# Filling TensorE's pauses at the start, and one low half moved from DVE to POOL at the end, in a recommendation tower

## The reference

```python
x0 = xk = e                                       # [b, 39, 16]
for idx, (W, b) in enumerate(params):             # W: (39, 39 or 64, 128)
    z = relu(einsum('bhd,bkd,hks->bsd', x0, xk, W) + b)
    # layers 0 and 1: xk = first 64 rows, the last 64 go to the output; layer 2: all 128
logit = sum(concatenate(direct, axis=1), axis=-1)  # [b, 256]
h = relu(concatenate([logit, dense_ctx]) @ W_top1 + b_top1)   # 272 -> 512
h = relu(h @ W_top2 + b_top2)                      # 512 -> 256
y = h @ W_top3
```

## Time and profile before

| | |
|---|---|
| median of 3 runs | 2482.67 us (2478.63, 2482.67, 2483.8) |
| the profiled execution | 2464.91 us, its span 2463.1 us |
| PE busy | 2416.9 us, 98% of the span, 8890 records |
| DVE busy | 2226.4 us, 90% |
| POOL busy | 1947.7 us, 79% |
| ACT busy | 1731.9 us, 70% |
| mean granted TensorE clock | 0.994 of full speed |

### The profile page before, as it was taken

One profiled execution on the slowest core, in us unless ns is written; L12 is line 12 of the kernel. 1 busy time (PEld: TensorE's weight loads), 2 busy tenths in 40 slices (PEclk: granted clock), 3 DMA queues, 4 the chain that ended last, 5 costly groups with the idle time before them and its releaser, 6 DMA issues.

```text
span 2463.1 us, 33434 instructions
## 1 busy us (share of the span) xinstructions
PE 2416.9 (98%) x8890; PEld 1646.8 (67%) x8890; DVE 2226.4 (90%) x1898; ACT 1731.9 (70%) x2202; POOL 1947.7 (79%) x1331
## 2 busy tenths in 40 slices
PE   6999999999999999999999999999999999999989
PEld 2566666666666666666666666666666666666656
DVE  1799999999989999999999999899999999999993
ACT  1677777777767777767777776676777777677655
POOL 6888888888878888888888888788887888866550
PEclk9899999999999999999999999999999999999999
DMA  3867766866766866776686677577678667767730
GB/s 76 182 140 157 165 136 140 175 140 136 163 139 128 172 146 137 155 162 139 138 175 139 138 161 158 118 163 154 137 148 174 134 139 168 148 138 150 164 93 1
DMA packets 214716, 352.60 MB, mean 143 GB/s; under 512 B 34382, under 2 KB 47566, under 8 KB 214588
## 3 DMA queue, kind: packets, MB, share of 16 engines
q1 hardware_dynamic: 194717, 347.07, 65.6%
q0 software_dynamic: 19968, 5.15, 2.2%
HBM read 346.97 MB, written 5.12 MB: 143 GB/s over the span
## 4 chain that ended last, share of the span: by engine, by line
PE 58%; POOL 24%; issue 13%; DVE 3%; ACT 1%; DMA 0%; POOLq 0%; SPq 0%; ACTq 0%; DVEq 0%
PE ps L929 22%; PE ps L939 11%; POOL Pl L422 11%; PE ps L919 10%; POOL emb L416 10%; PE ps L907 8%; PE ps L902 3%; POOL dir L451 2%; DVE P L764 1%; POOL sqx L428 1%; DVE ps L764 1%; PE ps L1056 1%; DVE Pl L769 1%; PE ps L895 1%; PE ps L1066 1%
## 5 line engine op out<-in xcount | busy, mean ns | idle before, releaser
L422 POOL TENSOR_TENSOR Pl<-P,Ph 128x1024 fp32r<-128x1024 f32 x448 | 1074.5, 2398 | 277.3 <-ACT Ph L566 268.8
L929 PE MATMUL ps<-Ph,wh 128*128 128x512 f32 x2048 | 965.0, 471 | 9.5 <-ACT Ph L566 9.5
L566 ACT ACTIVATE Ph<-ps 128x1024 fp32r<-128x1024 f32 x576 | 590.3, 1025 | 406.8 <-DVE ps L764 399.2
L764 DVE TENSOR_TENSOR P<-xb,ps 128x1024 f32<-128x1024 f32 x704 | 854.6, 1214 | 5.1 <-DMA xb<-x_dram 5.1
L769 DVE TENSOR_TENSOR Pl<-ps,Ph 128x1024 fp32r<-128x1024 f32 x576 | 705.4, 1225 | 112.8 <-ACT Ph L566 95.3
L929 PE MATMUL ps<-Ph,wl 128*128 128x512 f32 x1920 | 755.5, 394 | 0.0
L939 PE MATMUL ps<-Pl,wh 128*128 128x512 f32 x2048 | 742.4, 444 | 8.4 <-POOL Pl L422 8.4
L416 POOL DMA_INDIRECT emb<-tbl_in,idx x624 | 596.3, 956 | 171.5 <-issue 146.6
L764 DVE TENSOR_TENSOR ps<-xb,ps 128x1024 f32<-128x1024 f32 x576 | 707.0, 1227 | 19.6 <-DMA xb<-x_dram 1.3
L566 ACT ACTIVATE Ph<-P 128x1024 fp32r<-128x1024 f32 x448 | 473.9, 1058 | 186.0 <-DVE P L764 167.6
L939 PEld LDWEIGHTS ps<-Pl,wh 128*128 128x128 f32 x2048 | 384.5, 189 | 200.9 <-issue 117.9
(11 more groups left out here) (94 smaller groups left out, 899.3 us busy)
## 6 DMA issues: line engine op xcount, KB each, us to landing
xb<-x_dram SPq DMA_DIRECT2D x1280, 256.0 KB, 6.8
emb<-tbl_in,idx POOLq DMA_INDIRECT x624
x_dram<-rows SPq DMA_DIRECT2D x64, 78.0 KB
xb<-w_in SPq DMA_DIRECT2D x16, 128.0 KB
xb<-wt_in SPq DMA_DIRECT2D x2, 512.0 KB, 4.7
xb<-dense_in SPq DMA_DIRECT2D x1, 768.0 KB, 5.2
wp<-w_in SPq DMA_DIRECT2D x4, 128.0 KB
xb<-w0a_in SPq DMA_DIRECT2D x1, 448.0 KB
```

Source lines behind the costliest of these rows:

```text
L422: pool.tensor_tensor(Pl[:, h_slot(ref, c, k)], P[:, p_slot(ref, c, k)], Ph[:, h_slot(ref, c, k)], ALU.subtract).then_inc(low_pool, 1)
L566: act.activation(Ph[:, h_slot(ref, c, k)], p, ACT.Copy).then_inc(rounded, 1)
L764: dve.tensor_tensor(p, xb[:, x], xk.unsqueeze(1).broadcast_to([128, 2, N]), ALU.mult)\
L929: pe.matmul(z_of(c, k), w[:, q, j, :], Ph[:, h_slot(ref, c, k), j, :], start=k in (L1B, L2) and i + j == 0, stop=False)
```

## The change

Three edits.

1. The loop at the start becomes 80 products of 128x128 instead of 38 of 128x512, and the same short products are also issued in the loop over g: `WARM_T[g]` = 1 and 4 behind the transposes, `WARM_S[g]` = 1 and 2 behind the first three sums.
2. For chunk 1, ACT copies `x2` before `rows_sb` as it does for chunk 0; TensorE waits for `first_x` before the first two sums and for `aux_read` only before the third, which overwrites `aux_ps`.
3. The last chunk gets its own letters: step 10 goes from V to G, step 11 from G to V, step 12 from V to G. So of its steps 10 to 19, DVE makes 4 low halves instead of 5 and POOL 5 instead of 4.

```diff
-WARM = 38
+WARM, WARM_T, WARM_S = 80, (1, 4), (1, 2)
 KIND = "GVPVGPVGVPVGVGVGVGVP"
+LAST_KIND = "GVPVGPVGVPGVGGVGVGVP"
...
+def kind(i, k):
+    return (LAST_KIND if i == CHUNKS - 1 else KIND)[k]
...
             act.wait_ge(rows_written, 16)
-            copy_x(0, AUX)
+            act.wait_ge(aux_ready, AUX + 1)
+            act.activation(x2[:, :], aux_ps[0:R2], ACT.Copy).then_inc(first_x, 1)
+            act.activation(rows_sb, aux_ps[0:NF], ACT.Copy).then_inc(rows_ready, 1)
+            act.wait_ge(rows_ready, 2)
+            act.sem_inc(aux_read, 1)
...
-            with pe.Fori(0, WARM // 2):
-                for i in range(2):
-                    pe.matmul(z1_ps[:, 0], wp[:, 0, 0, :], wp[:, 0:2].rearrange("p q j m -> p (q j m)"), start=True, stop=True)
-
+            def repeat(n):
+                for i in range(n % 2):
+                    pe.matmul(z1_ps[:, 0, 0:S], wp[:, 0, 0, :], wp[:, 0, 1, :], start=True, stop=True)
+                if n < 2:
+                    return
+                with pe.Fori(0, n // 2):
+                    for i in range(2):
+                        pe.matmul(z1_ps[:, 0, 0:S], wp[:, 0, 0, :], wp[:, 0, 1, :], start=True, stop=True)
+
+            repeat(WARM)
...
                 transposes(g)
-                if g:
-                    pe.wait_ge(aux_read, READS + 1)
-                else:
-                    pe.wait_ge(first_x, 1)
+                repeat(WARM_T[g])
+                pe.wait_ge(first_x, g + 1)
                 for i, t in enumerate((FULL0, 0, 1)):
-                    if i == 2 and not g:
-                        pe.wait_ge(aux_read, 1)
+                    if i == 2:
+                        pe.wait_ge(aux_read, READS * g + 1)
                     sums(t, early_ps[g][i])
+                repeat(WARM_S[g])
```

More of the change, by code:

```diff
@@ L69 @@
                                              if not (i == CHUNKS - 1 and L1B <= k < L2)]
+def kind(i, k):
+    return (LAST_KIND if i == CHUNKS - 1 else KIND)[k]
+assert all((a == "P") == (b == "P") for a, b in zip(KIND, LAST_KIND))
 def counts(kinds):
@@ L76, in counts @@
         for k in range(STEPS):
-            n += KIND[k] in kinds and (i, k) in STEPSET
+            n += kind(i, k) in kinds and (i, k) in STEPSET
             table[i, k] = n
@@ L83 @@
 STEP, SPLITS, ONPOOL, ONDVE, PLAINS, STORED = (counts(kinds) for kinds in ("GVP", "GV", "G", "V", "P", "GP"))
-STORED_STEPS = [o for o in ORDER if KIND[o[1]] != "V"]
+STORED_STEPS = [o for o in ORDER if kind(*o) != "V"]
 SPLIT_STEPS = [o for o in ORDER if KIND[o[1]] != "P"]
@@ L483, in tile @@
                     for k in range(STEPS):
-                        if KIND[k] == "G" and (CPT * ref + c, k) in STEPSET:
+                        if kind(CPT * ref + c, k) == "G" and (CPT * ref + c, k) in STEPSET:
                             low(T, ref, c, k)
@@ L564, in round_ @@
                     act.wait_ge(split_done, upto(T, ref, SPLITS, *user))
-                p = P[:, p_slot(ref, c, k)] if KIND[k] == "G" else p_ps
+                p = P[:, p_slot(ref, c, k)] if kind(CPT * ref + c, k) == "G" else p_ps
                 act.activation(Ph[:, h_slot(ref, c, k)], p, ACT.Copy).then_inc(rounded, 1)
@@ L754, in product @@
                 p = p_ps
-                if KIND[k] != "V":
+                if kind(CPT * ref + c, k) != "V":
                     p = P[:, p_slot(ref, c, k)]
                     user = p_user(ref, c, k)
-                    if user and KIND[user[1]] == "G":
+                    if user and kind(CPT * ref + user[0], user[1]) == "G":
                         dve.wait_ge(low_pool, upto(T, ref, ONPOOL, *user))
@@ L845, in tile @@
                             low(*waiting)
-                        waiting = (T, ref, c, k) if KIND[k] == "V" else None
+                        waiting = (T, ref, c, k) if kind(CPT * ref + c, k) == "V" else None
                     if waiting:
@@ L933, in low @@
                 q = SPL.index(k)
-                if KIND[k] == "G":
+                if kind(CPT * ref + c, k) == "G":
                     pe.wait_ge(low_pool, upto(T, ref, ONPOOL, c, k))
```

## The result

| | before | after |
|---|---|---|
| median of 11 runs each | 2481.60 us (2478.63 to 2483.80) | 2491.06 us |
| ratio of after to before, 95% interval, the disturbed run left out | | 1.0034 [1.0024, 1.0043] |
| the profiled execution, its span | 2464.91, 2463.1 us | 2489.37, 2487.5 us |
| mean granted clock | 0.994 | 0.988 |

The change makes the kernel slower by 0.34%. Of the runs after, ten lie between 2486.66 and 2493.44 us; one of 3521.93 us, at a clock of 0.654, was disturbed and is left out of the ratio. The forecast was 2481.6 us, in a range of 2475.5 to 2486.0, so in effect no change.

The account below looks back on a forecast made before the run. PE was taken to bound the dense span, POOL's fixed list the start, and DVE the end, with POOL replacing it. Start 0.3 plus end 0.8 us, 1.1 off 2482.67, gave 2481.6 us, range 2475.5 to 2486.0.

Parts of the forecast that it names:

- The median as profiled time plus 17.76 us: Whole kernel: the runs' median was taken to stay 17.76 us above the profiled time after the change, as before.
- The loop of 80 "ends at 54.8 us": Ahead of the embeddings: 80 short products at 0.4 us end before the transposes at 57.37 us, costing nothing.
- the 59.5: Start: a loop ahead of the embeddings ending beyond 59.5 us would show the prediction wrong.
- the warm loop outlasts the gathers: Rival, start: weight loads in series make a product 0.60 us, the loop ends at 70.7: 2492.8 us, chance 0.05.
- Nearly all of the start's gain turns into a wait for POOL: Before step 0's low half: PE rests from 89.3 to 91.4 us for POOL, leaving 0.3 us of some 7.
- The pauses' products hold the clock: Chunks 0 and 1: short products fill PE's pauses at no cost, clock at 1.00 from 57 to about 89 us.
- The rival in which the clock falls in a new pause: PE's 2.1 us rest at 89 us lowers the clock, costing 1.7 us: 2483.3 us, chance 0.20.
- the start's gain carried: Rival, start: PE keeps 2.1 us (2479.5 us, 0.15) or all 7 us (2474.8 us, 0.05); chance 0.20 together.
- carried to the end unchanged: PE's dense stretch from 103.7 to 2329.5 us: whatever the start gains or loses passes through it to the end.
- x ahead of rows: Chunk 1: rows_sb and SP's write and spreads come 0.6 us later behind x, but covered, so cost nothing.
- The end, 0.8 us: Last chunk: DVE's 1.2 us saving brings the MLP only 0.8 us sooner, as POOL becomes the bound.
- The rival in which the end gains nothing: Last chunk: DVE's subtract holds POOL's last low half for 1.1 us: 2482.4 us, chance 0.07.

Follow-up runs that it names:

- e1: The kernel before, unchanged, on a chip with slow issue: 2481.16 us (one run).
- e18: The kernel before with only 20 of the first tile's 39 gathers, the other fields a constant, on a chip with slow issue: 2460.01 us, ratio 0.9913.
- e6: The changed kernel without its loop ahead of the embeddings, on a chip without slow issue: 2464.20 us, 0.9999 of before.
- e3: The changed kernel with the old loop of 38 products of 128x512, on a chip with slow issue: 2480.06 us, 0.9995 of before.
- e13: The kernel before, unchanged, on a chip without slow issue: 2464.43 us.
- e8: The changed kernel, its loop replaced by 8 products of 128x512 waiting for an increment behind POOL's 35th gather; no slow issue: 2464.21 us, 0.9996 of before.
- e9: The changed kernel, unchanged, run again on a chip with slow issue: 2487.30 us, 1.0028 of before.
- e10: The changed kernel without its loop ahead of the embeddings, on a chip with slow issue: 2466.26 us, 0.9941 of before.
- e11: The kernel before with only the last chunk's letters changed, on a chip with slow issue: 2479.36 us, 0.9998 of before.
- e17: The changed kernel, unchanged, run again on a chip with slow issue: 2488.94 us, 1.0031 of before.
- e2: The changed kernel with its 80 short products written out instead of looped, on a chip with slow issue: 2486.50 us, 1.0021 of before.
- e12: The kernel before with 16 instead of 38 products of 128x512 in its loop, on a chip with slow issue: 2468.62 us, 0.9956 of before.

## Why the prediction was wrong, step by step

**The median as profiled time plus 17.76 us: this step failed.** "I take the same difference off it" treats the difference as a constant around the kernel. It was a stall inside the loop ahead of the embeddings, the very place where the change doubles the records from 76 to 160. Runs of this kernel on one chip lie 4 to 6 us apart, so 17.76 us between a profile and the median asked for a cause before a sum was set on it. The kernel before has two times, medians of 2464.2 to 2464.5 and of 2479.8 to 2481.6 us. All runs of e1 to e18 on one chip agree in kind, but each chip was used at one time only, so whether it is the chip or the hour that decides is not shown.

**The loop of 80 "ends at 54.8 us": this step failed too, and it carries the loss.** It was costed at nothing; it put the transposes at 84.58 us, beyond the 59.5 that the prediction itself had named as the sign of being wrong. A short product was priced at 0.4 us, between 0.22 and 0.44. Where it is issued freely at full clock it costs 0.24 (3.73 us for 31 records), and the eight records behind chunk 1's transposes have 1.06 us in all. The rule that the prediction set beside it (the Trainium skill, TensorE: Matmul & The Clock Gate, Back-to-back issue gap, 81 ns) was the nearer one, if short of the 0.12 us that the trace shows. Freely issued the loop would end near 42 us, an estimate (22.4 + 160 x 0.12); here it ended at 84.5, since what counted was the number of records that still stood in line at 60.8 us, for which the sum had no term. The reading of 0.22 us a record as the half-clock price was right (26 records in 5.70 us).

**The rival "the warm loop outlasts the gathers" is what happened,** and its 2492.8 us lies near 2491.1, but by luck. Its mechanism, loads in series at 0.60 us a product, is refuted by the 0.12 us a record; and its argument against itself, that loads run beside products everywhere, was right and had no bearing.

**The account of the loss**, the profile of after against e1, the kernel before with slow issue too:

| stage | e1, us | after, us | difference |
|---|---|---|---|
| start to chunk 0's transposes | 75.81 | 84.58 | +8.77 |
| to chunk 2's transposes | 30.26 | 29.20 | -1.06 |
| to ACT's copy ahead of the last chunk's products | 2292.79 | 2294.11 | +1.32 |
| to the MLP's first product | 21.53 | 20.83 | -0.70 |
| to the end of the span | 58.91 | 58.78 | -0.13 |
| sum | 2479.3 | 2487.5 | +8.2 |

**"Nearly all of the start's gain turns into a wait for POOL": right, in e6,** where nothing precedes the start. Its timelines of PE and of POOL; they answer to the earlier trace rows.

```profile
87.88 0.60 PE L907 MATMUL ps<-ident,emb 128*78 128x128 f32 x4
...
91.90 0.72 PE L951 MATMUL ps<-Pl,wh 128*128 128x512 f32 x2 [1.80 <-POOL Pl L430]
```

```profile
78.47 2.38 POOL L430 TENSOR_TENSOR Pl<-P,Ph 128x1024 fp32r<-128x1024 f32 x1
...
89.47 2.38 POOL L430 TENSOR_TENSOR Pl<-P,Ph 128x1024 fp32r<-128x1024 f32 x1
```

PE reaches chunk 2's transposes 1.38 us earlier than before (87.88 against 89.26), then waits 1.80 us (predicted 2.1) and takes the low half at 91.90, where before took it at 91.48. POOL's two low halves start 0.4 to 0.6 us later than before, with no rest ahead of them: its list did not shorten. The gain predicted for the start was 0.3 us; none came: the low half is taken 0.42 us later.

**The pauses' products hold the clock: right for the pause behind chunk 1's transposes.** In e6, by stretch (columns as in the earlier trace rows):

```profile
70.00:80.00 10.00, 7.71 (x33) 4.99 (x33) 7.95 (x8) 7.56 (x13) 8.15 (x8) 1.00 0.75 158
...
92.00:104.00 12.00, 12.00 (x41) 7.55 (x41) 8.49 (x8) 7.89 (x12) 10.01 (x8) 1.00 0.85 170
```

The fall of 70.88 to 81.10 us is gone, and the new pause of 1.80 us lowers nothing behind it. The durations agree with the column: PE's three sums behind the pause take 1.16 us here and 1.56 in before. The early x and the products come together in every run, so which of the two does it is not separated. The rival in which the clock falls in a new pause (0.20) isn't refuted in general, and e3, with all of the change but its loop, shows it in the next chunk (below). e13, the kernel before, happened on the same pause, in its timeline of PE,

```profile
91.26 0.89 PE L939 MATMUL ps<-Pl,wh 128*128 128x512 f32 x2 [1.80 <-POOL Pl L422]
91.95 3.45 PE L919 MATMUL ps<-P,wp 128*128 128x512 f32 x4
```

and there four records took 3.45 us instead of 1.88. A rest of 1.46 us in e8 had no such cost. What decides is not shown.

**Is the start's gain carried (0.20)? Not here.** Where slow issue has made the start late, POOL's gathers are long over, the low half of step 0 waits for ACT (idle 2.88 us ahead of 113.56 in after) and the change does shorten the start: from chunk 0's transposes to chunk 2's 27.55 us in e3 against 30.26 in e1. Yet e3's time is that of before. It is given back in the next chunk, so "carried to the end unchanged" is wrong too. The timeline of PE, chunk 2's and chunk 3's transposes, in e1:

```profile
106.07 0.60 PE L895 MATMUL ps<-ident,emb 128*78 128x128 f32 x4
142.40 0.60 PE L895 MATMUL ps<-ident,emb 128*78 128x128 f32 x4
```

and in e3:

```profile
103.55 0.60 PE L907 MATMUL ps<-ident,emb 128*78 128x128 f32 x4
...
111.77 0.50 PE L941 MATMUL ps<-Ph,wh 128*128 128x512 f32 x1 [1.45 <-ACT Ph L574]
...
122.60 0.50 PE L941 MATMUL ps<-Ph,wh 128*128 128x512 f32 x1 [0.64 <-ACT Ph L574]
...
144.78 0.60 PE L907 MATMUL ps<-ident,emb 128*78 128x128 f32 x4
```

36.3 us in the one and 41.2 in the other. Of these 4.9 us, 2.3 are rests of PE (0.20, 1.45 and 0.64 us), where e1 has none, and some 1.6 are clock: behind the rest of 1.45 us the column falls to 0.57 from 112 to 116 us, and the eleven records from 111.77 to 116.41 us take 4.64 us where the same ones from 122.60 to 125.65 take 3.05. That is the rival of the clock, near its price of 1.7 us, in a pause that the prediction did not foresee. e3 by stretch (columns as in the earlier trace rows):

```profile
110.00:112.00 2.00, 0.55 (x3) 0.23 (x2) 1.84 (x3) 1.34 (x2) 0.20 (x1) 1.00 1.10 207
112.00:116.00 4.00, 4.00 (x10) 2.61 (x10) 2.37 (x2) 0.41 (x2) 3.56 (x3) 0.57 1.07 205
```

PE's waits point to ACT's rounding, and behind that stands DVE, in e3:

```profile
114.53 1.23 DVE L776 TENSOR_TENSOR ps<-xb,ps 128x1024 f32<-128x1024 f32 x1 [1.39 <-DMA xb<-x_dram]
117.11 1.22 DVE L776 TENSOR_TENSOR P<-xb,ps 128x1024 f32<-128x1024 f32 x1 [1.35 <-DMA xb<-x_dram]
```

The products come at the pace of SP's spreads from DRAM, 2.6 us apart, and meanwhile the DMA engines are full: e3 shows a share of 1.06 to 1.10 from 103.5 to 118 us, at 196 to 225 GB/s. The prediction named POOL's list as the one thing that a faster PE runs into; the spreads are a second. This reading rests on single profiles of e1, e3, e9 (38.9 us) and after (38.1 us); no run was made to test it. What x ahead of rows costs or gains by itself ("nothing") was not measured either.

**The end, 0.8 us: right in size and cause.** From ACT's copy ahead of the last chunk's products to the MLP's first product it is 21.52 us in before and 20.83 in after, 0.7 us. 20.80 to 20.85 us stand in e3, e6, e10 and e11. The timelines of POOL, DVE and PE in after; they answer to the earlier trace rows.

```profile
2410.88 4.76 POOL L430 TENSOR_TENSOR Pl<-P,Ph 128x1024 fp32r<-128x1024 f32 x2 [5.62 <-ACT Ph L574]
2415.58 1.31 POOL L459 TENSOR_TENSOR dir<-dir 128x512 f32<-128x512 f32 x1
...
2423.50 2.42 POOL L430 TENSOR_TENSOR Pl<-P,Ph 128x1024 fp32r<-128x1024 f32 x1
```

```profile
2424.95 2.04 DVE L876 TENSOR_TENSOR dense<-xb,dense 32x1024 fp32r<-32x1024 f32 x1
```

```profile
2428.72 0.40 PE L1070 MATMUL ps<-dense,emb_h 96*128 96x512 f32 x1
```

POOL has no rest between 2410.88 and its last low half, so it has taken DVE's place as the bound. DVE's subtract beside that low half took 2.04 us instead of 1.22, and POOL's low half kept its 2.42: **it is DVE that is held, not POOL,** whose operation had started first, and the same two durations stand in e3, e6, e9, e10 and e11 (2.01 to 2.06, 2.40 to 2.42 us). The rival in which the end gains nothing (0.07) falls. Below what a median tells, as forecast: e11, this edit alone, 0.9998.

**Left open.** The whole change was never run on a chip without slow issue: after and its repeats e9 and e17 all landed on chips with it. From e6 and from the price of a short product it should equal before there; that is argued, not shown. Open are also the path from the gathers to the issue of PE and ACT, how many gathers it takes, and what makes one chip (or one hour) differ from another.

## What to carry to other kernels

Put a number on the gap between a profiled execution and the median before a sum rests on it, and find the place of the gap in the trace; a gap beyond the runs' scatter is a stage that the profile didn't show. Work that only fills a wait is queued ahead of real work on an in-order engine: count its instructions as well as its time, let it end well before the input comes, and try the kernel without it, since here that version is 13.5 us ahead where issue is slow and loses nothing where it isn't. Behind a wait that is filled or shortened, look for every fixed list that feeds the stage (POOL's gathers, SP's transfers), not just the first.

## What the runs showed of the hardware

- Three of the five chips of e1 to e18 show PE's slow issue in the kernel's first 61 us: after 31 to 44 records of the loop one record each 2.0 to 2.8 us on average, single distances of 0.7 to 3.5, until 60.1 to 60.9 us, in kernels with loops of both shapes and in one without a loop instruction (e2). It costs the kernel before 15 to 17 us (medians) and the kernel after more. With 20 instead of 39 gathers in POOL's first list the wide loop doesn't show it (e18). ACT is hit as well: its copy of x waits until 60.81 us in e12, and its square until 88.93 us in e10.
- In e8 the semaphore increment behind POOL's gathers reached PE at 35.1 us, while POOL's timeline has the 35th gather, behind which the program puts it, at 49.09 to 50.03 us: the increment ran some 14 us ahead of that record.
- The clock column and the records can disagree. In e6, after a rest of 34.7 us, the column has 1.00 from 57.70 us on, but the four transposes there take 1.04 us instead of 0.60 and the records have half-clock durations up to 64 us; e8 shows the same durations with 0.50 beside them, and of e6's eleven runs four have a mean clock of 0.989 to 0.990 and seven 0.997, while their times overlap (2463.29 to 2464.20 and 2462.43 to 2466.19 us). Where they differ, the distance of the records is the better clock.
